# Attention block on one core: every projection in 128x32 strips ahead of the product with v, the transposes in other places, one VectorE reduction per score chunk

## The reference

```
h = x @ W1 + b1                      # q, k, v of 16 heads, 8 wide
w = softmax(q k^T / sqrt(8), causal)
x = layernorm(x + (w v) @ Wp + bp)
xr, xk = mu * x + (1 - mu) * x_prev  # x_prev: the token before
out = sigmoid(xr Wr^T) * (relu(xk Wk^T)^2 Wv^T)
x = layernorm(x + out)
```

## Time and profile before

| what | value |
|---|---|
| time, median of 3 runs | 714.41 us (711.55 to 716.44) |
| the profiled execution | 715.99 us, span 714.3 us |
| mean granted TensorE clock | 0.944 |
| PE busy | 599.9 us (84%) |
| DVE busy | 530.4 us (74%) |
| ACT busy | 464.6 us (65%) |
| POOL busy | 439.0 us (61%) |

### The profile page before, as it was taken

How to read it: one execution, slowest core, us unless ns; L and a number is a source line. 1 busy time by engine, 2 the same in 40 slices (tenths; PEclk the granted TensorE clock), 3 DMA queues, 4 the chain that set the end, 5 groups by cost and what they waited for, 6 DMA issues and landing times.

```text
span 714.3 us, 19231 instructions
## 1 busy us (share of the span) xinstructions
PE 599.9 (84%) x7405; PEld 321.4 (45%) x7405; DVE 530.4 (74%) x1388; ACT 464.6 (65%) x918; POOL 439.0 (61%) x680
## 2 busy tenths in 40 slices
PE   2359997999999999998989999899999998988623
PEld 1025453545454545454545454454545454533311
DVE  3058887889898888888898989797988888832121
ACT  1210776686878787778687777778687767676410
POOL 6110434467677676868676858576767767667653
PEclk9995899999999999999999999999999999989655
DMA  1332323132322323232323232415142332000100
GB/s 56 86 94 89 106 65 108 44 120 49 97 86 66 118 62 122 62 121 62 121 55 121 52 112 62 109 46 135 48 104 79 66 102 64 18 17 17 31 15 15
DMA packets 63615, 53.63 MB, mean 75 GB/s; under 512 B 8730, under 2 KB 59292, under 8 KB 63524
## 3 DMA queue, kind: packets, MB, share of 16 engines
q1 hardware_dynamic: 63524, 52.41, 26.2%
HBM read 34.82 MB, written 17.30 MB: 73 GB/s over the span
## 4 chain that ended last, share of the span: by engine, by line
PE 35%; POOL 25%; DVE 13%; ACT 11%; issue 10%; DMA 3%; SPq 2%; POOLq 0%; DVEq 0%; ACTq 0%
PE ops L537 9%; PE sps L493 7%; POOL probs L777 6%; PE spare L399 6%; ACT probs L616 5%; DVE rowmax L687 5%; POOL rstd L799 4%; POOL h L804 4%; POOL result L804 4%; PE spare L413 3%; PE spare L407 3%; PE tps L473 2%; POOL step_d L811 2%; DVE qk_rest L715 2%; DVE stats L698 2%
## 5 line engine op out<-in xcount | busy, mean ns | idle before, releaser
L616 ACT ACTIVATE probs<-tps 128x512 f32<-128x512 f32 x640 | 341.7, 598 | 125.6 <-PE tps L473 125.4
L687 DVE TENSOR_REDUCE rowmax<-sps 128x1 f32<-128x512 f32 (+2 forms) x768 | 337.7, 503 | 53.8 <-PE sps L507 52.0
L777 POOL TENSOR_SCALAR_AFFINE_SELECT probs<-probs 128x512 f32<-128x512 f32 x256 | 157.7, 633 | 157.5 <-ACT probs L616 157.0
L493 PE MATMUL sps<-kop,qop 52*128 52x384 bf16 (+3 forms) x1024 | 220.2, 310 | 34.3 <-DMA kop<-d_parts 13.8
L473 PE MATMUL tps<-qop,kop 54*128 54x128 bf16 (+3 forms) x1024 | 219.5, 304 | 12.6 <-ACT probs L616 12.6
L537 PE MATMUL ops<-probs,vop 128*32 128x384 f32 (+3 forms) x2048 | 172.7, 444 | 8.7 <-POOL probs L777 6.3
L493 PEld LDWEIGHTS sps<-kop,qop 52*128 52x128 bf16 x1024 | 71.3, 95 | 158.3 <-DVE rowmax L687 86.5
L505 PE MATMUL sps<-qmask,rows_of 64*128 64x128 bf16 (+1 forms) x640 | 134.3, 212 | 0.0
L507 PE MATMUL sps<-qmask,rows_of 64*128 64x128 bf16 (+1 forms) x640 | 131.8, 208 | 0.0
L691 DVE TENSOR_REDUCE rowmax<-sps 128x2 f32<-128x512 f32 x128 | 79.5, 684 | 13.7 <-PE sps L507 12.7
L537 PEld LDWEIGHTS ops<-probs,vop 128*32 128x32 f32 x2048 | 55.3, 110 | 73.1 <-issue 46.0
(11 more groups left out here) (75 smaller groups left out, 650.0 us busy)
## 6 DMA issues: line engine op xcount, KB each, us to landing
d_parts<-qk_parts SPq DMA_DIRECT2D x16, 768.0 KB, 3.9
qop<-d_parts SPq DMA_DIRECT2D x192, 32.0 KB
qop<-d_parts SPq DMA_DIRECT2D x64, 96.0 KB
kop<-d_parts SPq DMA_DIRECT2D x192, 32.0 KB
kop<-d_parts SPq DMA_DIRECT2D x64, 96.0 KB
xa<-L_attn_x SPq DMA_DIRECT2D x16, 256.0 KB, 3.0
xres<-L_attn_x SPq DMA_DIRECT2D x16, 256.0 KB, 3.4
out<-result SPq DMA_DIRECT2D x16, 256.0 KB, 2.5
```

Of the source, the lines that this page charges most:

```text
L493: nc.tensor.matmul(sps[:, bank(n), off:off + w], qop[r, par, pair, BLK * a:BLK * a + BLK], kop[r, par, pair, 0:w], start=j == 0, stop=Fals ...
L616: nc.scalar.activation(probs[:, g % 2, i, :], tps[:, bank(4 * GROUPS * n + 4 * g + i), :], ACT.Exp, scale=SCALE)\
L687: last = nc.vector.reduce_max(rowmax[:, par, QUARTET * half + t, hh, a:a + 1], sps[:, bank(n), off:off + w], axis=AX_X)
L777: last = nc.gpsimd.affine_select(out=v, in_=v, compare_op=ALU.is_ge, fill=0.0, base=0, pattern=[[0, QUARTET], [1, BLK]], channel_multiplie ...
```

## The change

Five things change. `gate` and `project` go in strips by tokens too, so the full-width helper is gone. The table of places is new: all seven projections stand ahead of a product with v, at (g, 1), and most transposes where there was room. VectorE reduces a short chunk in one instruction with four outputs, one for each 128 keys; for that `rowmax` has a further dimension, and block 0 comes first in the chunk. The three partial maxima of block 2 are combined once per half, by one small reduction after chunk 1 of iterations 4 and 9, which the `rowmax` transposes wait for (`block2_done`). The four multiplications into `attn` become one. And the moments of `z` go to iteration 7 and POOL's `z` to iteration 6, after the new place of `value`.

```diff
@@ SPARE_USES (two rows of the table)
-    (2, 0): ("E", "key"), (2, 1): ("D", "sums1"),
+    (2, 0): ("D", "sums1"), (2, 1): ("E", "key"),
...
@@ max_unit
-            return [(t, 2, 0, 3 * BLK), (t, 0, 3 * BLK, BLK)]
+            return [(t, 0, 0, BLK), (t, 2, BLK, 3 * BLK)]
@@ diagonals
-        return ap[:, (2 if u % 2 else 3) * BLK:].rearrange("p (j w) -> p j w", w=BLK)
+        blocks = ap.rearrange("p (j w) -> p j w", w=BLK)
+        return blocks[:, 0:NQBLK:3] if u % 2 else blocks[:, 3:]
@@ tensors
-        rowmax = sb("rowmax", [P, 2, PAIRS, 2, NQBLK])
+        rowmax = sb("rowmax", [P, 2, NQBLK, PAIRS, 2, NQBLK])
@@ TensorE
-            def tokens_by_weights(tokensT, weights):
-                for t in range(TT):
-                    last = nc.tensor.matmul(spare[:, P * t:P * t + P], tokensT[:, P * t:P * t + P], weights,
-                                            start=True, stop=True)
-                return last
...
                     wait(pe, s_reduced, 4 * GROUPS * before("S", b) + 2 * GROUPS)
+                    wait(pe, block2_done, 2 * before("S", b) + 1)
                     last = rowmax_transpose(1 - par, 0)
@@ VectorE, reduce_chunk
+                pair = QUARTET * half + max_unit(u)[0][0]
+                if u >= 2 * QUARTET:
+                    last = nc.vector.reduce_max(rowmax[:, par, 0, pair:pair + 2, hh, 1],
+                                                sps[:, bank(n), :].rearrange("p (j w) -> p j w", j=2), axis=AX_X)
+                elif u % 2 == 0:
+                    last = nc.vector.reduce_max(rowmax[:, par, 0, pair, hh, 3:], sps[:, bank(n), :], axis=AX_X)
                 else:
+                    last = nc.vector.reduce_max(rowmax[:, par, :, pair, hh, 0],
+                                                sps[:, bank(n), :].rearrange("p (j w) -> p j w", w=BLK), axis=AX_X)
                 last.then_inc(s_reduced, 1)
+                if c == CHUNKS - 1 and i == 1:
+                    wait(dve, s_reduced, n - 1)
+                    of = rowmax[:, par, :, QUARTET * half:QUARTET * half + QUARTET].rearrange("p j t h a -> p a (t h) j")
+                    nc.vector.reduce_max(of[:, 2, :, 0], of[:, 0, :, 1:], axis=AX_X).then_inc(block2_done, 1)
@@ VectorE, sums0 and sums1
-                    for t in range(TT):
-                        last = nc.vector.tensor_tensor(
-                            attn[:, t, DH * half:DH * half + DH].rearrange("q (r h) d -> q r h d", h=2),
-                            tiles[:, 0, t], inv[:, half, t].unsqueeze(3).to_broadcast([P, QUARTET, 2, DH]), ALU.mult)
-                    last.then_inc(spare_read, 1)
+                    nc.vector.tensor_tensor(
+                        attn[:, :, DH * half:DH * half + DH].rearrange("q t (r h) d -> q t r h d", h=2), tiles[:, 0],
+                        inv[:, half].unsqueeze(4).to_broadcast([P, TT, QUARTET, 2, DH]), ALU.mult).then_inc(spare_read, 1)
@@ VectorE, moments of z
-                    if g == 6 and active("E", b):
+                    if g == 7 and active("E", b):
@@ POOL, z
-                    if g == 5 and active("E", b):
+                    if g == 6 and active("E", b):
```

More of the change, by code:

```diff
@@ L232, in block_program @@
         s_reduced = sem("s_reduced")
+        block2_done = sem("block2_done")
         max_high = sem("max_high")
@@ L393, in rowmax_transpose @@
             def rowmax_transpose(par, half):
-                src = rowmax[:, par, QUARTET * half:QUARTET * half + QUARTET].rearrange("p t h a -> p (t h a)")
+                src = rowmax[:, par, 0, QUARTET * half:QUARTET * half + QUARTET].rearrange("p t h a -> p (t h a)")
                 return nc.tensor.transpose(spare[0:MAXIMA, 0:P], src, ident)
@@ L401, in weights_by_tokens, with tokens_by_weights @@
                 return last
-            def tokens_by_weights_in_strips(tokensT, weights):
+            def tokens_by_weights(tokensT, weights):
                 for t in range(TT):
@@ L428, in spare_use @@
                 elif use == "v":
-                    last = tokens_by_weights_in_strips(xT[:, 1 - par], w1p[:, 2, :])
+                    last = tokens_by_weights(xT[:, 1 - par], w1p[:, 2, :])
                 elif use == "max0":
                     wait(pe, s_reduced, 4 * GROUPS * before("S", b) + 2 * GROUPS)
+                    wait(pe, block2_done, 2 * before("S", b) + 1)
                     last = rowmax_transpose(1 - par, 0)
@@ L434, in spare_use @@
                     wait(pe, s_reduced, 4 * GROUPS * (before("T", b) + 1))
+                    wait(pe, block2_done, 2 * (before("T", b) + 1))
                     last = rowmax_transpose(par, 1)
@@ L457, in spare_use @@
                     wait(pe, ksq_done, before("E", b) + 1)
-                    last = tokens_by_weights_in_strips(ksq, wffT[:, 2, :])
+                    last = tokens_by_weights(ksq, wffT[:, 2, :])
                 last.then_inc(spare_written, 1)
@@ L684, in reduce_chunk @@
                 wait(dve, s_done, n + 1)
-                if u < 2 * QUARTET:
-                    for t, a, off, w in max_unit(u):
-                        last = nc.vector.reduce_max(rowmax[:, par, QUARTET * half + t, hh, a:a + 1],
-                                                    sps[:, bank(n), off:off + w], axis=AX_X)
-                else:
-                    pair = QUARTET * half + max_unit(u)[0][0]
-                    last = nc.vector.reduce_max(rowmax[:, par, pair:pair + 2, hh, 1],
-                                                sps[:, bank(n), :].rearrange("p (j w) -> p j w", j=2), axis=AX_X)
+                pair = QUARTET * half + max_unit(u)[0][0]
[4 more added lines that the diff above has]
+                    last = nc.vector.reduce_max(rowmax[:, par, 0, pair, hh, 3:], sps[:, bank(n), :], axis=AX_X)
+                else:
+                    last = nc.vector.reduce_max(rowmax[:, par, :, pair, hh, 0],
+                                                sps[:, bank(n), :].rearrange("p (j w) -> p j w", w=BLK), axis=AX_X)
                 last.then_inc(s_reduced, 1)
+                if c == CHUNKS - 1 and i == 1:
+                    wait(dve, s_reduced, n - 1)
+                    of = rowmax[:, par, :, QUARTET * half:QUARTET * half + QUARTET].rearrange("p j t h a -> p a (t h) j")
+                    nc.vector.reduce_max(of[:, 2, :, 0], of[:, 0, :, 1:], axis=AX_X).then_inc(block2_done, 1)
             def layer_norm_moments(src, i, n, ready, value, done_stats, done_moments):
```

## The result

The changed kernel takes 721.85 us (median of 4, 720.23 to 722.54) where the kernel before takes 715.04 (median of 4, 711.55 to 716.44): ratio 1.0126, 95% interval 1.0098 to 1.0154. It is slower by 1.3% by this ratio, and by 1.0% by the two medians (1.0095); 721 had been forecast, with 0.38 for slower by over 1%. The profiled execution took 720.23 us, span 718.5 us, against 715.99 and 714.3. TensorE's granted clock is 1.00 through all full steps of both, and 0.964 against 0.944 in the mean, so the loss isn't the clock's.

What follows compares the result with a forecast made beforehand. TensorE and VectorE were both taken as near their limit, with the order of VectorE's reads deciding. Eleven full steps at +0.8 plus 1.1, less 2, 0.8 and 0.7 outside, gave +6.4 on 714.4: 721 us, range 704 to 728.

Steps and rivals of the forecast that it cites:

- eight terms of a full step: Changes in TensorE's time in iterations 0, 2, 3 and 5 to 9, from -0.98 to +0.84 us each.
- iteration 2: `sums1` ahead of `key`: TensorE waits 0.6 us for VectorE's `attn`, so the product starts 0.50 us later.
- The sum of +0.94: All terms of a full step added: each full step becomes 0.94 us longer.
- the cut to +0.8 by hand: Full step's +0.94 us lowered to +0.8, since VectorE's reduced work may take a little from each wait.
- (1): Rival: TensorE sets the pace and the new waits have cover; 702 us, or 708 at half size; chance 0.22.
- (2): Rival: POOL's chain is the bound and hides TensorE's waits; +0.4 us a step, 716 us; chance 0.23.
- (3): Rival: a four-output reduction costs 0.83 us like its two parts, not 0.68; 736 us; chance 0.05.
- The wait of iteration 6: `max0` waits 0.69 us until VectorE has read `value` for `gated`; the iteration grows by 0.84 us.
- The 4.83 us: VectorE's work from iteration 5's first chunk through `gated`, before `max0` may write; TensorE itself needs 4.14 us.
- The bound on POOL's chain: From iteration 6's mask to `scaled`: with `gated` that late, the period could not fall below +0.4 us.
- the two steps with nearly all and the drain: Outside the eleven full steps: +1.1 us for two nearly complete steps, -0.7 us for draining.
- The first step with `project`: `project` moves under TensorE's 3.54 us wait at iteration 3's product for POOL's mask: -2 us.

Runs made afterwards that it cites:

- the mended order: Changed kernel with `key` ahead of `sums1`, `hT` and `sums0` at old places, `gated` ahead of the moments of `y`, early `xres` load: 701.3 us, period 37.18.
- strips and relief together: Changed kernel with old table and moments, keeping strips and VectorE's single instructions, with the early `xres` load: 708.2 us, ratio 0.9921 to the kernel before.
- VectorE's part alone: Kernel before with only the four-output reduction, the combining reduction and the single multiplication into `attn`: 714.4 us, ratio 1.0018.

## Why the prediction came out

**Right.** The forecast of 721 us held, with the mechanism and the place of each wait. Of the eight terms of a full step seven are good to 0.05, and iteration 2 is 0.10 too large: `key` starts 1.92 us after `sums1` and not 1.99, since VectorE got to `attn` that much sooner, and the rest is roundings and the product. The sum of +0.94 was 0.2 too large; the cut to +0.8 by hand was a guess at what VectorE's relief takes, and +0.75 was measured. Also as written: step 38.21, the waits for `attn` and `gated` of 0.6 each, the one for `rowmax` (1.07 forecast, 1.03 from start to start), the wait for ScalarE from 0.7 to 0.2, strips at 0.90, `attn` at 0.42, chunks at 0.68. That the places cause the loss is shown by undoing them (period 37.43) and by doing them alone (39.20).

**Rivals.** (1), that TensorE sets the pace and the waits have cover, fell: all waits are there, and `key` alone gives 0.42 back when undone. (2), the POOL chain as bound, is half right, and for the kernel before: with VectorE's work reduced there the period did not fall, 37.52, which agrees with POOL as the bound of that stretch and doesn't prove it. In the changed kernel POOL fell to 5% of the chain. (3) fell with the 681 ns of the four-output reduction.

**Wrong in a reason.** The wait of iteration 6 was priced at 0.69 as one for `gated`. The price held, the cause is wider: with `gated` sooner it moved to the next chunk at nearly the same size. The 4.83 us in the sum were right as a sum of VectorE's work from iteration 5's first chunk on. It was wrong to hang that on the one instruction that TensorE asks for. The bound on POOL's chain "as long as `gated` is that late" was not what held: `z` came sooner in that run (its wait for `gated` fell from 17.2 to 4.4 us in all), and the period stayed. By the traces POOL's chain was a second bound just behind VectorE's backlog: the 0.23 us of the mended order came only when both had moved.

**Mis-sized.** Outside the full steps: the two steps with nearly all and the drain were put at +1.1 - 0.7 = +0.4, and measured -0.78. From `key` to `key` the two steps took 35.88 and 37.39 before and take 36.24 and 35.49 now. The forecast has no term for the 1.9 us of the second. This step took 35.49 with strips at the old places and the early load too, 37.54 without the strips, but 37.21 with strips and relief together; what sets it stays open. The first step with `project` was put at -2 and gave -1.59. The doubled price of `project` was counted as saved (it took 2.08 us before, at a granted clock of 0.5 from 125.0 to 128.4); but the stretch at 0.5 is still there, from 123.9 to 127.3, and slows the chunks and the product instead (1.60 us for 1.05). The fill was put at -0.8 for VectorE's reductions and gave -0.87, which is in part luck: with VectorE's part alone `q` of step 1 starts at 106.19 and not sooner than before (106.12), and in the run with `gated` sooner, whose instructions up to there are those of the changed kernel, it starts at 104.07 and not 105.25. And the eleven full steps gave +7.44 where 11 x 0.75 = 8.25, because the DMA waits of `xres` fell differently (1.46 us in two steps after, 39.09 and 38.78, and 2.3 us in five before, 38.80 the longest). These waits were seen in the average of the earlier trace rows and in the earlier trace rows, but no term or range was set for how they would change; with strips alone they cost 6 us by the ratio and 8 by the medians with no order changed (721.1 against 713.2). In all +6.4 was forecast, and +4.2 by the spans and +6.8 by the medians measured, so that hitting 721 is in part luck. The forecast's own range is uneven as well: +0.6 to +1.0 a step gives 718 to 723 by its own sum, and not 727. The result lies 0.25 us above the 721.6 that the prediction took as the bound of 1%, so that the chances of 0.44 and 0.38 could not be told apart by the forecast.

## To carry to other kernels

In a pipeline of in-order engines, a wait for a named instruction is often the face of a backlog: sum what the releasing engine does since it last stood idle, because moving the named instruction alone can leave the time where it is (38.21 us both times), and pay only when the rest of the backlog is gone. Put the second engine's extra reads apart, one for each stretch in which it has caught up, before making any of them cheaper: the same cheaper instructions were worth 0.63 us a step in one order and none in another. And look in each engine's queue, the DMA issuer's too, for a load that stands behind a wait it doesn't need; moving one load gave 0.8%.

## What the hardware showed unexpectedly

The 256 KB load of `xres`, issued at its old place, landed between 3.1 and 5.3 us after its issue in the full steps of these programs. The late landings were more frequent in some programs than in others (in eight of eleven full steps with strips at the old places, 4.25 to 5.00). A store of 768 KB (`d_parts`) is issued some 1.65 us behind it in the kernel before, with VectorE's part, with strips and with `key` first, 2.0 in the changed kernel and 2.2 with the places alone. The distance doesn't sort the landings, since the kernel before and the one with strips share it. Whether the two share an engine or a memory path, and why a change of matmul shapes moves the landing, was not tried and stays open. Issued ahead of `load_max` the load lands 2.8 to 5.4 us after its issue, with as much scatter, but it no longer holds anything up.

A reduction of 512 columns from PSUM takes 684, 685 and 681 ns with one, two and four outputs a row: the number of outputs, up to four, costs nothing that shows.
